# Four graph layers on one core: the edge weight's term of the first layer moved from TensorE to VectorE, and the table of biased node rows moved from VectorE to GpSimd

## The reference, cut to what matters

```python
# layer 0
ef      = concat([x[src], x[dst], edge_weight[:, None]])       # 257 columns
msg     = leaky_relu(ef @ W_edge + b_edge)                     # slope 0.01
red     = segment_sum(msg, dst)
x       = layernorm(x + leaky_relu(concat([x, red]) @ W_node + b_node))
# layer 1: two attention convolutions (8 heads of 16), the first:
h       = relu(softmax-weighted sum over edges of v[src]  +  x @ s_w0 + s_b0)
# the second, and the residual of the layer
x       = layernorm(x + (... of h ...)  +  h @ s_w1 + s_b1)
```

## Time and profile before

| what | value |
|---|---|
| device time, median of 3 runs | 3342.61 us (3339.86 to 3343.45) |
| the profiled execution: from its first to its last instruction | 3538.4 us |
| PE busy in it | 2701.9 us (76%) |
| DVE busy | 2616.7 us (74%) |
| ACT busy | 2012.3 us (57%) |
| POOL busy | 1863.6 us (53%) |
| layer 0 | from about 137 to 697 us of that execution |
| first convolution | from about 703 to 1221 us |

### The profile page before, as it was taken

One profiled execution on the slowest core, in us unless ns is written; L12 is line 12 of the kernel. 1 busy time (PEld: TensorE's weight loads), 2 busy tenths in 40 slices (PEclk: granted clock), 3 DMA queues, 4 the chain that ended last, 5 costly groups with the idle time before them and its releaser, 6 DMA issues. The chain is left out here.

```text
span 3538.4 us, 46258 instructions
## 1 busy us (share of the span) xinstructions
PE 2701.9 (76%) x14325; PEld 1792.3 (51%) x14325; DVE 2616.7 (74%) x3171; ACT 2012.3 (57%) x3400; POOL 1863.6 (53%) x1771
## 2 busy tenths in 40 slices
PE   7799999689999778878785789999999774332332
PEld 3466666466666545555553246666666553221221
DVE  6589999889999868888884269999999994222322
ACT  0167777556665558878784258888888782111111
POOL 4477787333333276766663654554453003666665
PEclk6699999899999989999997899999999996566655
DMA  6357666556666556666662156666666653222221
GB/s 202 100 173 222 212 221 220 189 176 197 197 202 199 160 167 207 210 207 208 197 205 74 47 159 172 188 196 193 183 194 174 183 171 107 58 64 63 74 69 39
DMA packets 474800, 573.34 MB, mean 162 GB/s; under 512 B 65347, under 2 KB 283133, under 8 KB 474431
## 3 DMA queue, kind: packets, MB, share of 16 engines
q1 hardware_dynamic: 412744, 457.19, 42.0%
q0 software_dynamic: 56480, 111.88, 11.6%
q10 hardware_dynamic: 5334, 1.32, 0.2%
HBM read 353.51 MB, written 220.55 MB: 162 GB/s over the span
## 5 line engine op out<-in xcount | busy, mean ns | idle before, releaser
L1292 POOL DMA_INDIRECT g_xd_xs<-table_x,dst_row x196 | 211.8, 1081 | 360.4 <-PE g_psT L1358 250.7
L1804 POOL DMA_INDIRECT f_xs<-table_x,src_row x196 | 192.0, 980 | 312.5 <-POOLq L1216 253.1
L775 POOL DMA_INDIRECT c_xs<-table_x,src_row x196 | 185.5, 946 | 303.9 <-PE c_psT L916 250.6
L765 POOL DMA_INDIRECT c_xs<-table_h,src_row x196 | 206.9, 1056 | 193.0 <-PE c_psT L909 94.0
L1867 ACT ACTIVATE f_reluT<-f_psY 128x512 f32<-128x512 f32 x49 | 29.3, 597 | 472.6 <-DMA table_x<-g_x3o 329.2
L497 POOL DMA_INDIRECT xs<-in_x,src_i x196 | 224.7, 1147 | 101.6 <-issue 54.0
L482 POOL DMA_INDIRECT xd<-in_x,dst_i x196 | 222.9, 1137 | 96.3 <-issue 47.9
L1811 POOL DMA_INDIRECT out<-f_xo,end_i x196 | 198.7, 1014 | 121.1 <-DVE f_xo L1904 61.6
L1292 POOL DMA_INDIRECT g_xd_xs<-table_x,src_row x196 | 218.6, 1116 | 59.8 <-issue 59.8
L765 POOL DMA_INDIRECT c_xd<-table_h,dst_row x196 | 200.8, 1025 | 59.8 <-issue 59.8
L1363 PE MATMUL g_psP<-w_center,g_turns 128*128 128x128 f32 x1568 | 197.1, 279 | 13.6 <-ACT g_turns L1492 9.1
(11 more groups left out here) (330 smaller groups left out, 8669.8 us busy)
## 6 DMA issues: line engine op xcount, KB each, us to landing
g_share<-shares SPq DMA_DIRECT2D x196, 192.0 KB
xn<-in_x SPq DMA_DIRECT2D x49, 512.0 KB
table_x<-xo SPq DMA_DIRECT2D x49, 512.0 KB
table_x1b<-xb SPq DMA_DIRECT2D x49, 512.0 KB
c_xn<-table_x SPq DMA_DIRECT2D x49, 512.0 KB
table_h<-c_xo SPq DMA_DIRECT2D x49, 512.0 KB
c_xn<-table_h SPq DMA_DIRECT2D x49, 512.0 KB
c_x1r<-table_x1b SPq DMA_DIRECT2D x49, 512.0 KB
```

What stands on the lines that cost most here:

```text
L765: pool.indirect_dma_start(out=quarters(rows[:, s, :])[j], out_offset=None, in_=table, in_offset=edge_index(columns, now.n, j)).then_inc(la ...
L775: pool.indirect_dma_start(out=quarters(xs[:, s, :])[j], out_offset=None, in_=table, in_offset=edge_index(h.src_row, now.n, j)).then_inc(sr ...
L1292: pool.indirect_dma_start(out=quarters(xd_xs[:, s, k, :])[j], out_offset=None, in_=table, in_offset=edge_index(columns, now.n, j)).then_in ...
L1804: pool.indirect_dma_start(out=quarters(xs[:, s, :])[j], out_offset=None, in_=table, in_offset=edge_index(h.src_row, now.n, j)).then_inc(sr ...
```

## The change

Layer 0: the product with `w_edge_row` (L610) is gone, and with it the zeroed tile `erow`. SyncE sends the 512 edge weights of a tile to all 128 partitions (`ew`, 256 KB instead of 2 KB). ScalarE writes `zb = psZ + b_edge` in place of `z01`. VectorE has two operations in place of one: `z = ew * w_edge_col + zb`, then `msg = max(0.01*z, z)`, and both read only SBUF. TensorE may overwrite psZ once ScalarE has read it (`zb_ready`), where it waited for VectorE before (`msg_ready`). SyncE's load of the edge weights waits for `z` instead of for TensorE's psZ.

`x1b`: VectorE's addition L750 and the store L566 leave layer 0. In the first convolution GpSimd adds `s_b1c` to the node rows that this stage loads anyway; it does so for tile n-1 after the four transfers of tile n. SyncE's load of the node rows waits for that addition two tiles back, and SyncE stores `x1b` ahead of its wait for the result.

Setup: one memset and one small operation fewer; `w_edge_col` is loaded as a column.

```diff
@@ setup
-            load(h.w_edge_row[0:1, :], io["w_edge_row"])
+            load(h.w_edge_col[:, :], io["w_edge_row"].rearrange("o p -> p o"))
-            nc.vector.memset(h.w_edge_row[:, :], 0.0)
-            link(nc.vector.tensor_scalar(h.x01b_edge[:, :], h.col("b_edge"), 0.01, None, ALU.mult))
@@ layer0, SyncE
-            sp.wait_ge(erow_zero, 1)
-                    wait(sp, z_ready, now.n - 1)
-                    sp.dma_start(erow[0:1, s, :], io["ew"][:, bass.ds(now.n * TILE, TILE)]).then_inc(erow_landed[s], 16)
+                    wait(sp, zw_ready, now.n - 1)
+                    sp.dma_start(ew[:, s, :], io["ew"][:, bass.ds(now.n * TILE, TILE)].to_broadcast([P, TILE])
+                                 ).then_inc(ew_landed[s], 16)
-                if g and a == 0:
-                    sp.wait_ge(xb_ready, g.n + 1)
-                    sp.dma_start(node_rows(io["x1b"], g.n), xb[:, g.slot, :, :]).then_inc(xb_stored[g.slot], 16)
@@ layer0, TensorE
-                    pe.wait_ge(erow_landed[now.slot], 16 * (now.half + 1))
-                    wait(pe, msg_ready, now.n)
+                    wait(pe, zb_ready, now.n)
-                    nc.tensor.matmul(psZ[:, 0, :], h.w["w_dst"][:, :], edgeT[:, e, 0, :], start=False, stop=False)
-                    nc.tensor.matmul(psZ[:, 0, :], h.w_edge_row[:, :], erow[:, now.slot, :],
-                                     start=False, stop=True).then_inc(z_ready, 1)
+                    nc.tensor.matmul(psZ[:, 0, :], h.w["w_dst"][:, :], edgeT[:, e, 0, :], start=False, stop=True).then_inc(z_ready, 1)
-                    wait(pe, msg_ready, old.n + 3 if now else STEPS)
+                    wait(pe, zb_ready, old.n + 3 if now else STEPS)
@@ layer0, ScalarE
-                    wait(act, msg_ready, now.n)
-                    nc.scalar.activation(z01[:, :], psZ[:, 0, :], ACT.Identity, bias=h.x01b_edge[:, :],
-                                         scale=0.01).then_inc(z01_ready, 1)
+                    wait(act, zw_ready, now.n)
+                    nc.scalar.activation(zb[:, :], psZ[:, 0, :], ACT.Identity, bias=h.col("b_edge")).then_inc(zb_ready, 1)
@@ layer0, VectorE
-            nc.vector.memset(erow[:, :, :], 0.0).then_inc(erow_zero, 1)
-                    dve.wait_ge(z01_ready, now.n + 1)
+                    dve.wait_ge(zb_ready, now.n + 1)
+                    dve.wait_ge(ew_landed[s], 16 * (now.half + 1))
+                    wait(dve, msg_ready, now.n)
+                    nc.vector.scalar_tensor_tensor(out=z[:, :], in0=ew[:, s, :], scalar=h.w_edge_col[:, :],
+                                                   in1=zb[:, :], op0=ALU.mult, op1=ALU.add).then_inc(zw_ready, 1)
+                    dve.wait_ge(zw_ready, now.n + 1)
                     wait(dve, red_ready, now.n)
-                    nc.vector.scalar_tensor_tensor(out=msg[:, :], in0=psZ[:, 0, :], scalar=h.col("b_edge"),
-                                                   in1=z01[:, :], op0=ALU.add, op1=ALU.max).then_inc(msg_ready, 1)
+                    nc.vector.scalar_tensor_tensor(out=msg[:, :], in0=z[:, :], scalar=0.01, in1=z[:, :],
+                                                   op0=ALU.mult, op1=ALU.max).then_inc(msg_ready, 1)
-                    if a3 == 0:
-                        dve.wait_ge(out_ready, g3.n + 1)
-                        wait(dve, xb_stored[g3.slot], 16 * g3.half)
-                        nc.vector.tensor_tensor(wide(xb[:, g3.slot, :, :]), wide(xo[:, g3.slot, 0:2, :]),
-                                                h.s_b1c[:, :]..., ALU.add).then_inc(xb_ready, 1)
@@ conv, GpSimd (first convolution only)
+                    if now:
+                        gather_rows(nc, pool, h, now, table, xs, src_landed, turned)
+                    if last:
+                        s = last.slot
+                        pool.wait_ge(node_landed[s], 16 * (last.half + 1))
+                        wait(pool, xb_stored[s], 16 * last.half)
+                        nc.gpsimd.tensor_tensor(wide(xb[:, s, :, :]), wide(xn[:, s, :, :]),
+                                                h.s_b1c[:, :]..., ALU.add).then_inc(xb_ready, 1)
@@ conv, SyncE (first convolution only)
                     wait(sp, turned, per_tile * (now.n - 1))
+                        wait(sp, xb_ready, now.n - 1)
                     sp.dma_start(xn[:, s, :, :], node_rows(table, now.n)).then_inc(node_landed[s], 16)
...
                 if last:
+                    sp.wait_ge(xb_ready, last.n + 1)
+                    sp.dma_start(node_rows(io["x1b"], last.n), xb[:, last.slot, :, :]).then_inc(xb_stored[last.slot], 16)
                     sp.wait_ge(out_ready, last.n + 1)
```

More of the change, by code:

```diff
@@ L570, in _ @@
             sp.wait_ge(last_landed, 32)
-            for s in range(2):
-                sp.wait_ge(xb_stored[s], 16 * tiles_in_slot(s))
         @block.tensor
@@ L810, in conv @@
         xe = None if layer else sb("xe", [P, 2, TILE])
+        xb = None if layer else sb("xb", [P, 2, 2, TILE])
         x1r = sb("x1r", [P, 2, 3, TILE]) if layer else None
@@ L868, in step @@
                     wait(sp, turned, per_tile * (now.n - 1))
+                    if not layer:
+                        wait(sp, xb_ready, now.n - 1)
                     sp.dma_start(xn[:, s, :, :], node_rows(table, now.n)).then_inc(node_landed[s], 16)
@@ L901, in _ @@
             all_stored(sp, node_stored, edge_stored)
+            if not layer:
+                for s in range(2):
+                    sp.wait_ge(xb_stored[s], 16 * tiles_in_slot(s))
         @block.tensor
```

41 lines of the change are left out of this document (20 added, 21 removed).

## The result

| | median of its runs | ratio to the kernel before, 95% interval |
|---|---|---|
| kernel before | 3342.47 us (3339.86 to 3343.45, 4 runs) | |
| changed kernel | 3394.89 us (3393.74 to 3399.54, 4 runs) | 1.0167 (1.0154 to 1.0179) |
| changed kernel, on another chip beside a before of 3337.93 us | 3389.99 us (3383.64 to 3396.34, 4 runs) | 1.0162 (1.0145 to 1.0179) |
| changed kernel, on a third chip beside a before of 3605.56 us | 3613.65 us (3602.32 to 3633.93, 10 runs) | 1.0016 (0.9985 to 1.0047) |

The change costs 52 us in the first two rows; 25 were forecast. In the third row no cost is clear of the noise.

What follows compares the result with a forecast made beforehand. Engine time was taken as the bound: TensorE, VectorE and GpSimd's gathers in layer 0, VectorE in the first convolution. Layer 0 +6 and first convolution +19 make +25 on 3342.6, so 3368 us, range 3332 to 3400.

Steps and rivals of the forecast that it cites:

- The block by the addition: First convolution: VectorE's two-tile read waits for GpSimd's whole addition, +0.40 us a step, times 47 steps = +19 us.
- its start beside `pre` and L1136: First convolution: GpSimd's addition starts at about 920.1, 10.2 us after `pre` ends, while VectorE runs one-SBUF-tile reads.
- which instruction it would hold: First convolution: VectorE's `drop` (L1143), two SBUF tiles, wanted 1.2 us after the addition starts.
- the length of the addition: First convolution: GpSimd's addition takes 2.1 us, bounded by 1.23 (stage cost 0) and 2.8 (+36 us).
- the walk: Layer 0: gathers followed through a 9.98 us step, held by VectorE's two-tile reads; 6 fit, 11.98 us a tile.
- the sum from tile 11 to tile 48: Layer 0: 12 x 9.98 + 25 x 11.2 = 400 us against 37 x 10.56 = 391, +9 us.
- the lead: Layer 0: GpSimd's gathers run some 27 us ahead of TensorE; 24 of it is used up after 12 steps.
- Upwards 6 a step nearly throughout, +20: Layer 0, upper bound of the steady part: only 6 gathers a step nearly to the end, +20 us.
- (c): Rival, chance 0.12: 6 gathers a step throughout layer 0 (+17), first convolution's addition 2.8 us or queue without gap (+36); 3395.
- I carry the same +25 to the median: Whole kernel: profiled execution 195.8 us above the median, these stages taken as unaffected; +25 added to 3342.6 gives 3368.
- (a): Rival, chance 0.20: GpSimd's addition in the first convolution holds up nobody; layer 0's +6 alone, 3349 us.
- (b): Rival, chance 0.15: faster; 7 gathers still fit a layer 0 step (below 1.47 us each), gaining 10 us; 3333.

Runs made afterwards that it cites:

- the timed addition: Changed kernel plus one wait: GpSimd's addition in the first convolution waits for `dropm` of the tile before; 3375.04 us, ratio 1.0116, on a chip of 3338 us.

## Why the prediction was half of the result

**The first convolution: right in mechanism, one term mis-sized.** Forecast +19, measured +25.6. The block by the addition, its start beside `pre` and L1136, and which instruction it would hold were all as written; `drop` is held in 38 and in 36 of the 49 steps of the two profiles. The term that was mis-sized is the length of the addition: 2.36 us, not 2.1. Put into the prediction's own sum, 9.03 + 10.2 + 2.36 = 21.59 for two steps, 10.80 for one, +0.54 times 47 = +25. The mean step of 48 is (1222.6 - 705.8)/48 = 10.77, against (1174.8 - 681.6)/48 = 10.28. The Trainium skill (GPSIMD Engine Reference, section 3.1 on elementwise cycle accounting) gives 4497 ns for twice the numbers; half of it, an estimate of 2.25 us, is nearer to the 2.36 measured than my estimate from the iota of the earlier trace rows. For the hold itself the Trainium skill (SBUF — State Buffer, on the two separate sides) says that an instruction of VectorE with two SBUF inputs and one of GpSimd that reads SBUF shut each other out for the whole of the first; the runs agree both ways, with `drop` at up to 2.52 us behind the addition, the addition at up to 3.06 us, and `drop` at 0.69 inside a fill that reads nothing.

**Layer 0: the walk right, its bookkeeping wrong in two places, and the base.** Forecast +6, measured +24.2. What held: 9.98 us a step, 6 gathers in it, 2.4 us of holds, TensorE waiting for rows afterwards, the last gather at 660, VectorE's new instructions at 0.74 and 0.69. The step that failed is the sum from tile 11 to tile 48: how long the lead lasts, and what a tile costs once it is gone. In detail:
- *"the same walk then gives steps of 10.6 to 11.8, 11.2 on average".* A step of 11.2 with 7 gathers is 1.60 us for each, which is what was measured: 1.59 and 1.57 behind the first long step. But a tile needs 7.2 gathers, as the prediction itself says three paragraphs up, and 7.2 x 1.59 = 11.4. Measured: 11.63 and 11.43 from the first long step to tile 48. Single steps are 9.98 or 10 to 18 us, not 10.6 to 11.8 each. Over the 25 steps that the prediction gave it, +6 to +11.
- *"The lead ... is gone after 24/2.0 = 12 steps. From tile 11".* The steps before tile 11 run at 9.98 too and use up the lead with it; the first long step is that of tile 12, not 23. Eleven steps at 11.4 to 11.6 in place of 9.98, +16 to +18.
- Against this, TensorE and VectorE reach tile 11 8.6 us sooner than before (257.2 against 265.8), of which the prediction had only the 1 us of the memset, and the end gives 2.6, where it had 2. In all, from tile 11 to tile 48: 421.6 us where 400 was forecast; in the kernel before 386.2, where the prediction had 391.
- *"Upwards 6 a step nearly throughout, +20."* The prediction's own 11.98 us a tile, put into its own sum, gives 12 x 9.98 + 25 x 11.98 = 419 against 391, +28. The upper bound was some 8 us too low by its own terms, and (c), which uses it, too.
- *"of which these stages show no sign; I carry the same +25 to the median".* Layer 0 of that execution ended at 703.0 us, and at 681.6 in one that takes the median's time. The sign was there: idle time of ScalarE ahead of L680 and L683 that nothing ends, 11.1 and 10.2 us in that profile's list of waits, all of it absent from the later profile of 3332.8 us. An irregular start of the stage (steps of 15.9, 14.6 and 12.8 us) made before look 21 us longer. My forecast of where layer 0 would end, 703 + 6, is within 4 us of where it ended, 705.8 and 711.7; that was luck: the base was 21 us too high and the cost 18 too low.

**The stages behind the first convolution**, for which the prediction has no term, cost nothing: -0.7 us. Right was also the price of the broadcast, the stores and the removed matmul: TensorE's part of the step did fall to 9.98, as the run with fewer gathers shows for nearly the whole stage.

**The rivals.** (a), that the addition holds up nobody, fell. (b) named the right lever, the length of a gather against 1.47 us: at 1.57 to 1.59 layer 0 is slower, at 1.43 it is faster, and the kernel with it by 14.6 us. (c) has the measured time, 3395, though not its parts (the addition is 2.36, not 2.8). The result lies inside the range, at its upper end.

## What to carry to other kernels

An engine that only issues transfers is a full engine when its time per tile is near the step, and its rate contains what the others hold from it: a shorter step of VectorE and TensorE was worth nothing here because each gather became 0.08 us dearer (1.57 against 1.49), and one instruction moved past another turned layer 0's loss of 24 us into a gain of 22. When work is given to GpSimd, ask which two-tile reads of VectorE it will meet, and let a wait put it beside instructions of VectorE that read PSUM; that took back 19 of 26 us. When a part of a change is run alone and costs as much as the whole, look at what sets the pace in each: here it was VectorE in the one and GpSimd in the other. Before a difference is carried from one profile to the median, check that the profiled execution is of the median's kind, by idle time that no event ends.

## What had not been expected

- A wait of TensorE for rows costs more than itself in its step: behind the wait of 3.64 us four matmuls took 3.41 us in place of 1.95, at a granted clock of 0.54.
- VectorE's instruction is recorded as started while it is held: `drop` shows as 2.52 us long and not as idle time ahead of it, so the list of waits names nobody, and only the spread of one instruction's length (691/1416/2519) shows the conflict.
- Which running sum is beside the addition matters. The backward fill (L1108, 1.27 us) takes its data from PSUM and is not lengthened; `den` (L1171) reads two SBUF tiles and is. The expectations of the timed addition had scans as safe without this difference.
